# Layer-norm and raw inputs of a cross-attention block transposed by block loads and VectorE instead of TensorE, with layer norm prepared a step ahead

## The reference

```python
# layer 0: H = 512, 16 heads of 32
ln_out = layernorm(x, ln1_s, ln1_b)                       # stage A: self attention
q, k, v = split(ln_out @ w_qkv + b_qkv)
x = x + merge(attention(q, k, v, ltor_mask)) @ w_ao + b_ao
ln_out = layernorm(x, ln2_s, ln2_b)                       # stage B: cross attention
q = ln_out @ w_q + b_q
k, v = split(encoder_states @ w_kv + b_kv)
x = x + merge(attention(q, k, v, cross_mask)) @ w_co + b_co
ln_out = layernorm(x, ln3_s, ln3_b)                       # the MLP
x = x + gelu(ln_out @ w1 + b1) @ w2 + b2
# layer 1, stage D: queries from x, keys and values from layernorm(context)
a = layernorm(ctx, gamma, beta)
out = attention(x @ Wq.T, a @ Wk.T, a @ Wv.T, mask) @ Wo.T
return x + tanh(gate) * out
```

## Time and profile before

| | us |
|---|---|
| median of 3 runs | 1181.85 (1181.65 to 1183.79) |
| the profiled execution, its own time | 1184.43 |
| span of the profiled execution | 1183.1 |
| PE busy | 1157.4 (98%) |
| PEld busy | 1039.4 (88%) |
| DVE busy | 795.5 (67%) |
| ACT busy | 723.3 (61%) |
| POOL busy | 419.5 (35%) |
| 16 DMA engines, queue of SP | 26.2% |

### The profile page before, as it was taken

How to read it: one execution, slowest core, us unless ns; L and a number is a source line. 1 busy time by engine, 2 the same in 40 slices (tenths; PEclk the granted TensorE clock), 3 DMA queues, 4 the chain that set the end, 5 groups by cost and what they waited for, 6 DMA issues and landing times.

```text
span 1183.1 us, 26625 instructions
## 1 busy us (share of the span) xinstructions
PE 1157.4 (98%) x10069; PEld 1039.4 (88%) x10069; DVE 795.5 (67%) x1345; ACT 723.3 (61%) x2450; POOL 419.5 (35%) x305
## 2 busy tenths in 40 slices
PE   7999999999999999899999999999999999999998
PEld 6889989889988889787899999999998889988886
DVE  6676666666776667788856656655667476666677
ACT  4677677677667776677433433434445486766766
POOL 3666655456555465557511202202201310111100
PEclk9999999999999999989999999999999999999999
DMA  5222222333333333334211011100214123223222
GB/s 201 82 64 91 91 82 73 90 96 107 105 109 108 94 103 113 97 107 143 82 36 54 19 37 32 41 36 19 90 37 142 57 65 92 91 67 92 79 67 85
DMA packets 60383, 96.92 MB, mean 82 GB/s; under 512 B 11504, under 2 KB 14816, under 8 KB 60256
## 3 DMA queue, kind: packets, MB, share of 16 engines
q1 hardware_dynamic: 60256, 95.22, 26.2%
HBM read 78.02 MB, written 17.16 MB: 80 GB/s over the span
## 4 chain that ended last, share of the span: by engine, by line
PE 87%; DVE 5%; issue 2%; ACT 1%; POOL 1%; DMA 1%; SPq 0%; DVEq 0%; ACTq 0%; POOLq 0%
PE psum L544 20%; PE psum L732 14%; PE psum L708 14%; PE psum L652 10%; PE psum L538 10%; PE psum L587 6%; PE psum L563 4%; PE psum L620 4%; PE psum L640 3%; DVE prob L1351 1%; DVE context_lo L1388 1%; ACT prob L1021 0%; DVE context_lo L1438 0%; DVE context_hi L1434 0%; DVE kT L1426 0%
## 5 line engine op out<-in xcount | busy, mean ns | idle before, releaser
L1021 ACT ACTIVATE prob<-prob,negmax 128x128 f32<-128x128 f32 x768 | 297.5, 397 | 26.7 <-DVE negmax L1364 26.6
L544 PE MATMUL psum<-inputs_hi,weights_hi 128*128 128x256 f32 x768 | 224.8, 293 | 1.2 <-DVE weights_lo L1644 0.8
L544 PE MATMUL psum<-inputs_lo,weights_hi 128*128 128x256 f32 x768 | 217.0, 283 | 0.0
L544 PE MATMUL psum<-inputs_hi,weights_lo 128*128 128x256 f32 x768 | 216.9, 282 | 0.0
L1727 POOL TENSOR_TENSOR prob<-prob,mask_bias 128x1024 f32<-128x1024 f32 x64 | 152.9, 2411 | 2.2 <-issue 2.1
L544 PEld LDWEIGHTS psum<-inputs_hi,weights_hi 128*128 128x128 f32 x768 | 146.6, 191 | 5.7 <-ACT qT L991 1.0
L1717 POOL TENSOR_TENSOR inputs_lo<-ln_tile,inputs_hi 128x512 fp32r<-128x512 f32 x64 | 89.4, 1416 | 174.5 <-DVE inputs_hi L1325 169.7
L1021 ACT ACTIVATION_READ_ACCUMULATOR prob<-prob,negmax 128x1 f32 x768 | 150.3, 196 | 0.0
L544 PEld LDWEIGHTS psum<-inputs_lo,weights_hi 128*128 128x128 f32 x768 | 147.0, 191 | 0.2
L544 PEld LDWEIGHTS psum<-inputs_hi,weights_lo 128*128 128x128 f32 x768 | 146.8, 191 | 0.0
L708 PE MATMUL psum<-inputs_hi,weights_hi 128*128 128x256 f32 x512 | 145.8, 285 | 0.0
(11 more groups left out here) (111 smaller groups left out, 2715.6 us busy)
## 6 DMA issues: line engine op xcount, KB each, us to landing
weights_raw<-weights_in SPq DMA_DIRECT2D x72, 256.0 KB, 3.1
stream<-residual SPq DMA_DIRECT2D x48, 256.0 KB, 2.1
ln_tile<-stream SPq DMA_DIRECT2D x48, 256.0 KB, 2.8
residual<-stream SPq DMA_DIRECT2D x48, 256.0 KB, 2.9
context<-row_sums_spread SPq DMA_DIRECT2D x188, 64.0 KB, 2.0
ln_tile<-enc_in SPq DMA_DIRECT2D x32, 256.0 KB, 2.9
ln_tile<-x_in SPq DMA_DIRECT2D x16, 256.0 KB, 3.1
residual<-x_in SPq DMA_DIRECT2D x16, 256.0 KB, 3.2
```

Of the source, the lines that this page charges most:

```text
L544: mm = pe.matmul(ps[:, bank, GT * part:GT * part + GT], w[:, slot, c, o], a[:, buf, c, :], start=c == 0 and i == 0, stop=c == KC - 1 and i ...
L1021: ins = act.activation(P[:, T * s:T * s + T], P[:, T * s:T * s + T], ACT.Exp, bias=negmax[:, par, s:s + 1], accum_out=total[:, par, s:s + 1])
```

## The change

Only the first two fills are still transposed on TensorE. The other 46 reach a new tile `xt` (features on partitions, 256 tokens) in one of two ways. Eight raw fills of the encoder come from a copy of the encoder input that is handed to the kernel already transposed, in one DMA. The other 38 are **turned**: four DMAs, one for each block of 32 partitions, place 32x32 blocks of the row-major source in `xt` in pieces of 32 floats (128 bytes), and one VectorE `transpose` turns all blocks in place. A turned layer-norm fill is normalised in `lnx`, stored to a tensor in memory (512 KB, two slots), and loaded back in blocks; a raw fill of D is loaded in blocks straight from the stream.

Layer norm is prepared earlier: statistics two steps ahead (`st.later`), `normalise` and the store one step ahead (`st.ahead`), the turn in the step of the fill. `xt` has one buffer: a load waits for the low part of the fill before. The low part of raw fills moves from VectorE to GpSimd. ACT's weight split moves from the next step into the step of its load, and ACT does the second half projection, the fill and `prob_out(2)` ahead of the exponentials. The third fill moves from step 0 to step 1.

```diff
-            if not odd and b < 12:
+            if b == 1 or (not odd and 0 < b < 12):
                 fill = ln_fill(0, q + 2, q % 2)
...
+    _next = [s.fill for s in STEPS[_p][1:] + (STEPS[B][:2] if _p == A else [])] + [None, None]
+    if _p == B:
+        _next[14] = mlp_fill(1)
+    STEPS[_p] = [s._replace(ahead=_next[i] if _p != A or i else None, later=_next[i + 1]) for i, s in enumerate(STEPS[_p])]
...
+TURNED = [fill for fill in FILLS[2:] if fill.ln is not None or fill.phase == D]
...
+        xt = sb("inputs_transposed", [128, KC, GT])
+        normal = nc.dram_tensor("normalised", (2 * GT, H), f32, kind="Internal").ap()
...
+            def store_normalised(fill):
+                n = LN_FILLS.index(fill)
+                sp.wait_ge(s_xhat, 2 * fill.n + 2)
+                if n >= 2:
+                    sp.wait_ge(s_xt, LANDED[LN_FILLS[n - 2]])
+                dst = normal[slot_rows(fill), :].rearrange("(t p) n -> p t n", p=T)
+                sp.dma_start(dst, lnx[:, :, :]).then_inc(s_nst, 16)
+
+            def load_transposed(fill):
+                was = PREVIOUS[fill]
+                if was in FILLS[:2]:
+                    pass
+                elif was.ln is None:
+                    sp.wait_ge(s_rlo, 2 * was.n + 2)
+                else:
+                    sp.wait_ge(s_flo, 2 * was.n + 2)
+                if fill not in TURNED:
+                    src = encT[:, bass.ds(fill.q * GT, GT)].rearrange("(c p) n -> p c n", c=KC)
+                    sp.dma_start(xt[:, :, :], src).then_inc(s_xt, 16)
+                    return
+                if fill.ln is not None:
+                    sp.wait_ge(s_nst, 16 * (LN_FILLS.index(fill) + 1))
+                    rows = normal[slot_rows(fill), :]
+                else:
+                    rows = source(fill)[bass.ds(fill.q * GT, GT), :]
+                blocks = rows.rearrange("(b t) (c a f) -> a t c b f", t=32, a=4, f=32)
+                for a in range(4):
+                    dst = xt[32 * a:32 * a + 32, :, :].rearrange("p c (b f) -> p c b f", f=32)
+                    sp.dma_start(dst, blocks[a]).then_inc(s_xt, 16)
...
```

In a step, SP:

```diff
-                if st.ahead and not st.fill:
-                    load_tiles(st.ahead)
+                ahead_ln = st.ahead and st.ahead.ln is not None
+                if st.later and st.later.ln is not None and not ahead_ln and g:
+                    load_tiles(st.later)
                 if st.prev:
                     store_row_sums(g - 1)
                     spread_row_sums(g - 1)
-                if st.ahead and st.fill and g > 0:
-                    load_tiles(st.ahead)
+                if ahead_ln:
+                    store_normalised(st.ahead)
+                if st.later and st.later.ln is not None and ahead_ln:
+                    load_tiles(st.later)
+                if st.ahead:
+                    load_transposed(st.ahead)
...
```

TensorE:

```diff
                     transpose_prob(g - 1, 0)
                     transpose_prob(g - 1, 1)
-                if st.fill and g:
-                    fill_transpose(st.fill, g)
...
```

ACT:

```diff
-                if was and was.weight and g > 2:
-                    split(was.weight)
...
+                regular = st.ends and st.units[2] and not late
+                if st.weight and g > 1:
+                    split(st.weight)
+                if st.fill and not regular:
                     fill_out(st.fill)
...
+                if regular:
+                    half_out(*st.units[1])
+                if st.fill and regular:
+                    fill_out(st.fill)
+                if regular:
+                    prob_out(g - 1, 2)
                 exps(g, 0)
...
```

VectorE has a new function:

```diff
+            def turn_inputs(fill):
+                dve.wait_ge(s_xt, LANDED[fill])
+                whole = xt[:, :, :].rearrange("p c n -> p (c n)")
+                dve.transpose(whole, whole).then_inc(s_xturn, 1)
...
```

And in a step:

```diff
                 if st.prev:
                     prob_out(g - 1, 1)
                 v_out(*st.units[0])
+                if st.ahead and st.ahead.ln is not None:
+                    normalise(st.ahead)
+                if st.fill in TURNED:
+                    turn_inputs(st.fill)
                 row_max(g, 0)
-                if st.fill and st.fill.ln is None:
-                    fill_split(st.fill)
+                if st.units[2]:
+                    v_out(*st.units[1])
                 row_max(g, 1)
-                if st.fill and st.fill.ln is not None:
-                    fill_split(st.fill)
                 if st.prev:
                     prob_out(g - 1, 3)
-                v_out(*st.units[1])
+                if st.fill and st.fill.ln is not None:
+                    fill_hi(st.fill)
...
-                if st.ahead and st.ahead.ln is not None and st.ahead != mlp_fill(0):
-                    if not early:
-                        statistics(st.ahead)
-                    normalise(st.ahead)
+                if st.later and st.later.ln is not None:
+                    statistics(st.later)
```

More of the change, by code:

```diff
@@ L42 @@
 Fill = namedtuple("Fill", "ln phase q buf n")
-Step = namedtuple("Step", "phase b prev ends units fill weight ahead")
+Step = namedtuple("Step", "phase b prev ends units fill weight ahead later")
 def ln_fill(ln, q, buf):
@@ L175, in gelu_buffer @@
     return 1 if p < 3 else (p + 1) % 2
+FILLS_OF_MLP = [None] + [mlp_fill(q) for q in range(2, NG)] + [ln_fill(3, 0, 1), ln_fill(3, 1, 1)]
 LAST_SPLITS = {2: (16, 0), 3: (16, 2), 4: (17, 0), 5: (17, 2), 6: (18, 0), 7: (18, 2)}
@@ L547, in project, with scores @@
                     mm.then_inc(s_half, 1)
-            def scores(g, before):
+            def scores(g):
                 phase, q, half, gp = g // 16, (g % 16) // 2, g % 2, (g // 2) % 2
@@ L755, in step @@
                     times_v(g - 2)
-                if g == 32:
-                    scores(g, ln_fill(3, 1, 1))
-                else:
-                    scores(g, was.fill if was and was.fill in STEP_FILLS else None)
+                scores(g)
                 if was and (was.units[2] or was.units[0]):
@@ L795, in last_steps_of_b @@
                     times_v(g - 2)
-                    scores(g, mlp_fill(0) if b == 14 else None)
+                    scores(g)
                     if b == 14:
@@ L1146, in last_steps_of_b @@
                     context_hi(g - 2, 1)
-                    if b == 14:
-                        split(STEPS[B][13].weight)
-                    else:
+                    if b == 15:
                         split(LATE[14][3])
@@ L1483, in step @@
                     inverse_sums(g - 1)
-                early = phase == A and not st.fill and st.ahead and st.ahead.ln is not None
-                if early:
-                    statistics(st.ahead)
-                if st.fill == mlp_fill(0):
-                    statistics(st.fill)
-                    normalise(st.fill)
                 if st.prev:
@@ L1522, in last_steps_of_b @@
                     prob_out(g - 1, 1)
+                    if b == 14:
+                        normalise(mlp_fill(1))
                     row_max(g, 0)
@@ L1656, in dve_program @@
             last_steps_of_b()
-            statistics(mlp_fill(1))
-            normalise(mlp_fill(1))
             for p in range(5, NG * NPAIR):
@@ L1667, in dve_program @@
                     gelu_lo(p - 1)
-                fill = mlp_fill(g + 1) if g < NG - 1 else ln_fill(3, 0, 1)
+                if jp == 0:
+                    statistics(FILLS_OF_MLP[g])
                 if jp == 1:
                     mlp_out(g - 1)
-                if jp == 2:
-                    statistics(fill)
-                if jp == 3:
-                    normalise(fill)
-                if jp == (5 if g == 0 else 4):
-                    fill_split(fill)
+                    normalise(FILLS_OF_MLP[g])
+                if jp == 4:
+                    turn_inputs(FILLS_OF_MLP[g])
+                if jp == 5:
+                    if g == 0:
+                        turn_inputs(mlp_fill(1))
+                    fill_hi(FILLS_OF_MLP[g] or mlp_fill(1))
+                if g == NG - 1 and jp == 3:
+                    statistics(ln_fill(3, 1, 1))
+                    normalise(ln_fill(3, 1, 1))
                 if g == NG - 1 and jp in LAST_SPLITS:
@@ L1749, in step @@
                     attention_residual(g - 2)
-                if st.fill and st.fill.ln is not None:
+                if st.fill:
                     fill_lo(st.fill)
-                if st.ahead and st.ahead.ln is not None and st.ahead != mlp_fill(0):
-                    inverse_deviation(st.ahead)
                 if g == 1:
@@ L1757, in step @@
                     split(st.weight)
+                if st.later and st.later.ln is not None:
+                    inverse_deviation(st.later)
             def last_steps_of_b():
@@ L1806, in pool_program @@
                 g, jp = divmod(p, NPAIR)
-                fill = mlp_fill(g + 1) if g < NG - 1 else ln_fill(3, 0, 1)
+                if jp == 0:
```

(9 more changed lines are left out.)

263 lines of the change are left out of this document (122 added, 141 removed).

## The result

| | before | after |
|---|---|---|
| median of the runs | 1182.07 us (4 runs) | 1165.94 us (4 runs, 1163.93 to 1167.59) |
| ratio, 95% interval | | 0.986 (0.984 to 0.988) |
| profiled execution: own time, span | 1184.43, 1183.1 us | 1163.93, 1162.6 us |

What follows compares the result with a forecast made beforehand. TensorE was taken as the bound, busy 1157.4 of 1183.1 us. 1184.4 - 45.3 + 6 (normalise) + 4 (load) = 1149.1, less 2.6 for the profiled run, gave 1146 us; range 1130 to 1190, likeliest case 1140 to 1158.

Steps and rivals of the forecast that it cites:

- What leaves TensorE: Transposes of 46 fills leave: 37 in attention or by a projection at 0.79 us, 9 in MLP at 0.87; gain 37.1 us.
- The stall in step 13: Step 13 of B: normalising one step ahead removes TensorE's idle and low clock; 6.2 us more gain, bounds 3 and 8.5.
- Normalise beside GpSimd: Odd steps of A and B: `normalise` during GpSimd's bias delays row maximum and exponentials; 6 us lost over 13 pairs.
- the fourth rival: `normalise` meets so much of GpSimd's bias that each of 13 pairs loses 2 us or more: 1166 us; chance 0.14.
- First groups of the MLP: TensorE's wait for VectorE shrinks as `statistics` and `normalise` move to B's steps 13 and 14; gain 1.5 us, bounds 0 and 3.5.
- Start of the kernel: Step 0 loses a fill; gain 0.5 us, bounds 0 and 1.
- The load: Block load of a turned fill: 4 us taken, up to about 5 free; 4 us lost in D and in shared queues.
- the first two rivals: Loads in A, B, D: 5 to 6.3 us (1174 us at 6.0), chance 0.16; or over 6.3 (1230 at 8), chance 0.17.
- The prediction's estimate from the Trainium skill: Block load priced as a 19 times slower transposing DMA: 6.2 us per fill, time then 1180 us, inside the first rival.
- VectorE's transpose: One 128x1024 turn for each of 38 fills on VectorE: 1.1 us, bounds 0.5 and 2.5; 42 us in all, hidden.

Runs made afterwards that it cites:

- run 1: Changed kernel, ScalarE's copy of the second unit and third quarter of the probabilities placed ahead of the turned fill's scaling; ratio to the kernel before 0.9824.
- run 2: Changed kernel, VectorE's `normalise` of the next step's fill moved ahead of the masking from the third step on; ratio to the kernel before 0.983.
- run 3: Changed kernel, both ScalarE copies (second unit, third quarter of probabilities) ahead of the fill's scaling, also in steps without a third unit; ratio to the kernel before 0.9813.
- run 6: Changed kernel with the edits of run 3 and run 4, and that of run 2 in A and B alone; 1150.89 us, ratio to the kernel before 0.9723.
- run 9: `no_d` with GpSimd's low parts of the weights of units 11 to 15 cut to 64 of 512 columns (output wrong); ratio to the kernel before 0.9687.
- run 5: Changed kernel, in steps 13 to 15 of B SyncE's next weight loads ahead of the prepared fill's store and load; ratio to the kernel before 0.9866.
- run 7: `no_d` with VectorE's fourth probability quarter ahead of the row maxima in A's step 1, second MLP fill's `normalise` ending B's step 14; ratio to the kernel before 0.9740.
- run 8: `no_d` with VectorE's turn of the first MLP fill ahead of the context's low parts in step 13 of B; ratio to the kernel before 0.9737.
- run 4: Changed kernel, block load of D's second layer-norm fill issued ahead of the last MLP residual's store on SyncE; ratio to the kernel before 0.9821.
- no_d: The kernel of run 6: changed kernel with three mends to the orders of ScalarE, VectorE and SyncE; 1150.89 us, ratio to the kernel before 0.9723.

## Why the prediction failed, point by point

**What leaves TensorE: right, the size a little low.** 0.87 us per fill in B and D (1.74 a pair) for 0.79, and 0.88 in the MLP for 0.87. The difference of starts in the earlier trace rows leaves out that the first matmul behind the transposes is itself longer (0.36 against 0.28 us). 46 fills give 40 us, not 37.1.

**The stall in step 13: the step that failed.** The prediction said: "The change normalises one step ahead, so the order becomes: wait for `prob_out(28, 1)`, the last two quarters' transposes, the output projection [...]. What is late next is `w1(0)`", with 6.2 us of gain and "No idle of 5.5 us and no low clock near 500". It followed the stall forward and not the work that was moved. `normalise(mlp_fill(0))` went into step 12, ahead of that step's turn and beside GpSimd's bias, where it takes 3.5 us; ScalarE's scaling waits for the turn; and in the steps without a third unit both copies that TensorE needs stand behind the scaling. The order that the prediction gives for ScalarE ("`half_out` of the second unit (ready at 9.1), the fill (1.9 us) and `prob_out`") is that of the other steps. Measured: -1.4 us for steps 12 and 13 against -7.3. Runs 1 to 3 and 6 show the two causes and that both must go for the whole of it: with them mended the two steps take 28.12 us. The rest of the miss is made of smaller ones at three other places, below.

**Normalise beside GpSimd (6 us, bounds 0 to 2 us for each of 13 pairs): the mechanism right, the place wrong.** 13 pairs took 3.06 to 3.77 us, as many as I had counted; of the other 18, 15 took 0.98 to 1.00 and three 1.96 to 2.34. In B's first twelve steps that costs nothing: ScalarE's exponentials, where I placed the loss, have the room. In A it costs 0.85 us a pair, by the copy of `v`. The room had been counted small: by the prediction's own figures it is 5.0 - 1.2 = 3.8 us, not 3.5. The measured time is that of the fourth rival (1166), and that is luck: its cause, 2 us in each of 13 pairs, is not what the runs show. VectorE's order is worth 3 us in A and 5.7 in steps 12 and 13 of B, and nothing in the other twelve steps of B.

**First groups of the MLP (a gain of 1.5 us, and two fills, 1.7).** Measured +1.8, a miss of 5 us. The term's own wait did shrink, from 1.77 to 0.60 us, but TensorE's waits of the stretch rose from 3.8 to 7.4 us in all, against 1.7 us of transposes that are gone. GpSimd's splits beside VectorE's GELU hold TensorE in the first groups (run 9). They met in the kernel before, too (waits of 0.17, 1.19, 0.66 and 1.77 us there; now 1.04, 1.19, 1.01, 1.19 and 0.60), so I take it that work taken from TensorE in this stretch had little to gain; that was not tried by itself. Steps 14 and 15 add 2.2 us of waits (1.00, 0.57, 0.26, 0.39); runs 5, 7 and 8 tried three orders there and none helped, so their cause stays open.

**Start of D (no term of its own; four fills less).** A miss of 6 us. The prediction listed what SyncE's queue holds within a step, and not what the new load is queued behind here. Run 4 gives 3.0 us back. `no_d` is still 4 short of the forecast, and 1.3 of these are the wait behind the late raw fill.

**Start of the kernel (+0.5 and two fills).** A miss of 4.5 us in steps 0 to 3: the fill moved from step 0 into step 1, where the turn, `normalise` and the scaling stand ahead of copies. Run 7 removes one of these waits and meets the next. How much of it can be had stays open.

**The load, the first two rivals (0.33 together): wrong in the steps, right at the start of D.** Of the 38 turns of the changed kernel three wait for their load (10.12, 0.65 and 0.54 us), all of them around the start of D; the steady steps have none. There the rivals' mechanism, VectorE idle until the load and TensorE idle behind it, is what the traces show, by the load's place in SyncE's queue and by its slow issue. The prediction had 1.74 us of issues, 4 of load and 2 to land, 7.7 in all; 5.3 us lie between the first issue and the turn where VectorE waits for it in run 4, and 8.2 where the four issues took 5.2. The issues are what was off most: 2.7 to 5.2 us for four, not 1.74 (as whole rows 1.7 to 3.1).

The prediction's estimate from the Trainium skill (VectorE: DVE Perf Modes, The three transpose paths) left out a condition: the page gives its 19 times for a large innermost stride of the destination. Here the innermost 32 floats lie in a row on both sides, so the rule says nothing of this load. No run tests it. What the small pieces cost can be worked out: (0.393 - 0.350) x 16 x 1162.6 = 800 us of engine time over 150,784 more packets are 5.3 ns each, 1.3 us per fill on 16 engines.

**VectorE's transpose (1.1 us, bounds 0.5 to 2.5): right.** 38 of them, all alike; beside it the 62 `normalise`:

```profile
L1334 DVE STREAM_TRANSPOSE inputs_transposed<-inputs_transposed x38: 1229/1234/1245, 53.9 to 1108.8; 128x1024 f32<-128x1024 f32 x38
```

```profile
L1327 DVE TENSOR_SCALAR ln_tile<-ln_tile,ln_mean_var,ln_rstd 128x512 f32<-128x512 f32 x62 | 64.6, 1082 | 4.6 <-POOL ln_rstd L1745 4.6
```

## What to carry to other kernels

When a change moves work to another engine, the steady step is the easy part: the gain is lost where the order of work differs (first and last steps, a stage without its third unit, the step that a stall used to pad). For each instruction that now waits for later data, list what stands behind it in its queue and who needs that, in every form of the step. And where a stall is removed, look one step earlier as well, at the place where the work that caused it now lies.

## What the runs showed of the hardware

VectorE's instructions split into two kinds beside GpSimd. `normalise` (two of 512 elements) took 1.00 us beside an idle GpSimd, 3.58 us beside its bias in A and 3.07 in most of B; the GELU's `TENSOR_SCALAR` 0.43 and 1.40, its subtraction 0.69 and 1.65. The row maximum (about 1.2, some of them beside the bias) and the transpose (1.23 to 1.25) did not change, though 13 transposes lay beside GpSimd's work for their whole length. That agrees with the Trainium skill, SBUF — State Buffer, Who interferes with whom: copies, casts and `tensor_scalar` can take a pair of ports that VectorE shares with GpSimd, operations with two SBUF inputs meet GpSimd's reads there, and a `tensor_reduce` doesn't. Where such an instruction stands in a step can be worth more than its length: moved ahead of the masking (6 us earlier in step 12 of B), 13 pairs of them cost VectorE 30 us less in all (64.6 to 34.4 in `no_d`).
